# One of 16 source-row tiles of each slot in the third edge stage: one-hot products on TensorE from a table in SBUF instead of an indirect DMA

## The reference, cut to what matters

```python
row, col = (edge_index[0], edge_index[1])          # src, dst; the edges are sorted by dst
m = jnp.concatenate([x[row], x[col], edge_attr], axis=1)
h = jnp.maximum(m @ W1 + b1, 0.0)
h = jnp.maximum(h @ W2 + b2, 0.0)
h = h @ W3 + b3
s = jax.ops.segment_sum(h, col, num_segments=n)
agg_max = jax.ops.segment_max(h, col, num_segments=n)
```

## Time and profile before

| | us |
|---|---|
| median of 3 runs | 12,724.05 |
| lowest and highest of them | 12,720.05 and 12,810.73 |
| the profiled execution, its own time | 12,744.54 |
| span of that execution, first to last instruction | 12,742.7 |
| mean granted clock of TensorE in it | 0.537 of 2.4 GHz |
| third edge stage in it, from its first instruction to its last product with `yg` | 8716.3 to 12,576.2 |

### The profile page before, as it was taken

How to read it: one execution, slowest core, us unless ns; L and a number is a source line. 1 busy time by engine, 2 the same in 40 slices (tenths; PEclk the granted TensorE clock), 3 DMA queues, 4 the chain that set the end, 5 groups by cost and what they waited for, 6 DMA issues and landing times. The chain is left out here.

```text
span 12742.7 us, 117881 instructions
## 1 busy us (share of the span) xinstructions
PE 2970.5 (23%) x12074; PEld 2055.6 (16%) x12074; DVE 6179.3 (48%) x21579; ACT 1252.9 (10%) x3613; POOL 9537.5 (75%) x9956
## 2 busy tenths in 40 slices
PE   2000011111100640000000000013545545545455
PEld 2000011111100320000000000012333333333334
DVE  8877477777743432222222222224555555555555
ACT  3111111111111330000000000000101001011001
POOL 7777777777777767777777777777777777777776
PEclk6555555555555775555555555555555555555556
DMA  6444444444444432222222222222222222222221
GB/s 168 120 118 116 115 127 117 118 116 118 116 119 115 127 120 74 66 66 74 66 70 66 66 66 72 68 52 55 68 67 67 67 68 67 67 67 67 67 67 49
DMA packets 766546, 1107.81 MB, mean 87 GB/s; under 512 B 277264, under 2 KB 383263, under 8 KB 765038
## 3 DMA queue, kind: packets, MB, share of 16 engines
q0 software_dynamic: 328208, 302.76, 12.8%
q1 hardware_dynamic: 257781, 569.91, 12.3%
q10 hardware_dynamic: 179944, 229.99, 6.1%
HBM read 548.77 MB, written 553.01 MB: 86 GB/s over the span
## 5 line engine op out<-in xcount | busy, mean ns | idle before, releaser
L137 POOL DMA_INDIRECT g<-in_edge_attr,idxs x3072 | 2955.4, 962 | 938.3 <-issue 857.1
L137 POOL DMA_INDIRECT yg<-ytab,idx x3077 | 2911.6, 946 | 949.4 <-issue 920.1
L137 POOL DMA_INDIRECT msg<-Y,idx x3025 | 2874.0, 950 | 984.8 <-issue 923.5
L1600 DVE SCALAR_TENSOR_TENSOR run<-run,same,msg 128x64 f32<-128x64 f32 x3125 | 891.0, 285 | 2910.9 <-DMA msg<-Y,idx 2803.4
L611 DVE SCALAR_TENSOR_TENSOR run<-run,sameD 128x80 f32<-128x80 f32 x3072 | 907.9, 296 | 1324.3 <-DMA g<-in_edge_attr,idxs 882.5
L2023 DVE SCALAR_TENSOR_TENSOR run<-run,same,ps 128x32 f32<-128x32 f32 x3125 | 774.7, 248 | 1584.1 <-PE ps L1917 1428.7
L1156 PE MATMUL ps<-tail,before 128*128 128x64 f32 (+2 forms) x10 | 2.8, 421 | 4456.5 <-PEq L1470 3811.3
L1901 PE MATMUL ps<-ident,zx 128*128 128x128 f32 x1564 | 524.8, 439 | 1460.6 <-DMA yg<-ytab,idx 1430.5
L2006 DVE SCALAR_TENSOR_TENSOR zx<-zx,same,zs 128x32 f32<-128x32 f32 x3124 | 793.4, 254 | 135.3 <-DVE anew L1989 28.6
L615 DVE SCALAR_TENSOR_TENSOR runS<-runS,sameS,g 128x64 f32<-128x64 f32 x3072 | 852.4, 277 | 0.1
L1000 PE MATMUL ps<-hot 128*98 128x128 bf16 x3072 | 373.1, 315 | 1816.3 <-DVE hot L718 1816.3
(11 more groups left out here) (356 smaller groups left out, 5893.0 us busy)
## 6 DMA issues: line engine op xcount, KB each, us to landing
R<-run SPq DMA_DIRECT2D x390, 320.0 KB, 2.3
msg<-Y ACTq DMA_DIRECT2D x6400, 0.2 KB
msg<-Y SPq DMA_DIRECT2D x6400, 0.2 KB
R<-run SPq DMA_DIRECT2D x195, 512.0 KB, 3.0
R<-run SPq DMA_DIRECT2D x124, 800.0 KB, 5.3
v<-in_edge_attr ACTq DMA_DIRECT2D x384, 256.0 KB
yg<-ytab SPq DMA_DIRECT2D x6144, 0.1 KB
RA<-runS SPq DMA_DIRECT2D x256, 256.0 KB, 2.9
```

Source lines behind the costliest of these rows:

```text
L137: eng.indirect_dma_start(out=out, out_offset=None, in_=table, in_offset=bass.IndirectOffsetOnAxis(ap=index, axis=0)).then_inc(sem, 16)
L1600: ins_ = v.scalar_tensor_tensor(out=run[:, q, t, :], in0=prev, scalar=same[:, q, t:t + 1], in1=msg[:, q, t, :], op0=ALU.mult, op1=ALU.add)
```

## The change

Tile 4 of each of the 192 full slots (`HOT3`) is no longer fetched by GpSimd. At the start of the stage the whole `ytab` is loaded into SBUF (partition p holds its 98 nodes as 98 x 32 floats), and VectorE splits each float into three bf16 parts whose sum is the float (`prepare`). The source node of an edge is written as 7 times a key plus a rest (`HB2` = 7); the key names one of 128 x 14 groups of 7 nodes. For each slot:

- VectorE copies the keys of the tile's 128 edges (`next_key`); TensorE spreads them over all partitions by one fp32 product (`spread_key`).
- VectorE compares them with each partition's 14 group numbers into `hot`, 128 x 1792 bf16 (`one_hots`).
- TensorE multiplies 14 one-hot matrices with the three parts of the table, 42 bf16 products of 128x128 by 128x224 into one bank (`find`).
- VectorE picks one of the 7 rows of each group: a mask, a product of 128 x 224 and a sum over 7 (`pick`), into `yg`.

The steps run ahead of the slot by written order. In turn n TensorE runs `slot(n)`, then `find` for slot n + 2, then `spread_key` for slot n + 4; VectorE runs its old turn n, then `pick` for n + 2, `one_hots` for n + 3, `next_key` for n + 4. Bank 1, the second bank of stage 0, is given to the new products, so stage 0 keeps one bank. The tail is as before.

The core of the diff:

```diff
@@ edges_3, GpSimd
                 for t in range(steps):
-                    if by_rows(c, q) and t == ROW_AT3:
+                    if within(c, q) and t == HOT3 or by_rows(c, q) and t == ROW_AT3:
                         continue
                     gather(pool, yg[:, q, t * MSG:(t + 1) * MSG], k.ytab, idx[:, q, t:t + 1], got[q])
@@ edges_3, TensorE
+                        if within(c, q):
+                            pe.wait_ge(y_picked, n + 1)
...
+            def spread_key(c, q):
+                pe.wait_ge(keyed, NS3 * c + q + 1)
+                nc.tensor.matmul(psK, key[:, 0:1].to_broadcast([P, P]), k.ident[:, :], start=True, stop=True)\
+                    .then_inc(key_spread, 1)
+
+            def find(c, q):
+                pe.wait_ge(hot_ready, NS3 * c + q + 1)
+                for i in range(HN):
+                    for part in parts_y:
+                        last = nc.tensor.matmul(psP, hot[:, i, :], part[:, i * HB2 * MSG:(i + 1) * HB2 * MSG],
+                                                start=i == 0 and part is parts_y[0], stop=i == HN - 1 and part is parts_y[2])
+                last.then_inc(y_found, 1)
+
             def body(c):
                 for q in range(NS3):
                     slot(c, q, SL3)
-
-            turns(pe, CHUNKS3, body)
+                    for work, m in ((find, 2), (spread_key, 4)):
+                        if within(*after(c, q, m)):
+                            work(*after(c, q, m))
+
+            spread_key(0, 0)
+            pe.wait_ge(parts_done, 1)
+            find(0, 0)
+            spread_key(0, 1)
+            find(0, 1)
+            spread_key(0, 2)
+            spread_key(0, 3)
+            body(0)
@@ edges_3, VectorE
+            def next_key(c, q):
+                copy_at(v, key[:, :], hot_key[:, bass.ds(NS3 * c + q, 1)]).then_inc(keyed, 1)
+
+            def one_hots(c, q):
+                v.wait_ge(key_spread, NS3 * c + q + 1)
+                v.tensor_tensor(hot[:, :, :], over(psK, 1, HN), over(place[:, :], 2, P), ALU.is_equal).then_inc(hot_ready, 1)
+
+            def pick(c, q):
+                s.done(v.tensor_tensor(mask[:, :], seq[:, :], hot_in[:, bass.ds(NS3 * c + q, 1)].to_broadcast([P, HB2]), ALU.is_equal))
+                v.wait_ge(y_found, NS3 * c + q + 1)
+                s.wait(s.n)
+                s.link(v.tensor_tensor(picked[:, :, :], psP.rearrange("p (b f) -> p b f", f=MSG), over(mask[:, :], 2, MSG), ALU.mult))
+                v.tensor_reduce(yg[:, q, HOT3 * MSG:(HOT3 + 1) * MSG], picked[:, :, :].rearrange("p b f -> p f b"), AX.X, ALU.add)\
+                    .then_inc(y_picked, 1)
+
+            def prepare():
...
+                next_key(0, 0)
...
+                v.wait_ge(y_loaded, 16)
+                s.link(v.tensor_copy(parts_y[0][:, :], ysb[:, :]))
+                s.link(v.tensor_tensor(y_rest[:, :], ysb[:, :], parts_y[0][:, :], ALU.subtract))
+                s.link(v.tensor_copy(parts_y[1][:, :], y_rest[:, :]))
+                v.tensor_tensor(parts_y[2][:, :], y_rest[:, :], parts_y[1][:, :], ALU.subtract).then_inc(parts_done, 1)
+                v.wait_ge(parts_done, 1)
+                one_hots(0, 0)
+                pick(0, 0)
+                next_key(0, 1)
+                one_hots(0, 1)
+                pick(0, 1)
+                next_key(0, 2)
+                one_hots(0, 2)
+                next_key(0, 3)
+
             def body(c):
                 s.fresh()
                 for q in range(NS3):
...
                     aggregate(c, q, SL3)
                     v.wait_ge(run_ready, NS3 * c + q + 1)
                     meta(c + 1, q)
+                    for work, m in ((pick, 2), (one_hots, 3), (next_key, 4)):
+                        if within(*after(c, q, m)):
+                            work(*after(c, q, m))
```

More of the change, by code:

```diff
@@ L65 @@
 SP_ROWS, ACT_ROWS = (1, 3), (2, 4)
+HN, HB2 = 14, 7
+HOT3 = 4
 BY_ROW = (1, 2, 3, 4)
@@ L416, in edges_01 @@
                             [Xf[:, 2 * CA + h * CA // 2:2 * CA + (h + 1) * CA // 2] for h in range(2)], ctx)
-        loaded, got, stored80, storedS = ([sem(f"{s}{q}") for q in range(NQ)]
-                                          for s in ("loaded", "got", "stored80_", "storedS"))
-        added = [sem(f"added{q}") for q in range(NTAB)]
+        loaded, stored80, storedS = ([sem(f"{s}{q}") for q in range(NQ)] for s in ("loaded", "stored80_", "storedS"))
+        got, added = k.left_got, k.added
         l_srcB, l_left, l_rest, l_dst, tabs_zero, settled, consts, wzero = (
@@ L1803, in edges_3 @@
                              "run_ready3", "vsteps3"))
+        ysb, y_rest = sb("ysb", [P, NB * MSG]), sb("y_rest", [P, NB * MSG])
+        parts_y = [sb(f"y_part{i}", [P, NB * MSG], BF16) for i in range(3)]
+        seq_i, place_i = sb("seq3_i", [P, HB2], I32), sb("place3_i", [P, HN], I32)
+        seq, place = sb("seq3", [P, HB2]), sb("place3", [P, HN])
+        hot_src, hot_key, hot_in = (sb(f"hot3_{s}", [P, NS3 * CHUNKS3]) for s in ("src", "key", "in"))
+        key, mask = sb("key3", [P, 1]), sb("mask3", [P, HB2])
+        hot, picked = sb("hot3", [P, HN, P], BF16), sb("picked3", [P, HB2, MSG])
+        y_loaded, seqs_made, keyed, key_spread, hot_ready, y_found, y_picked, parts_done = (
+            sem(s) for s in ("y_loaded3", "seqs_made3", "keyed3", "key_spread3", "hot_ready3", "y_found3", "y_picked3",
+                             "parts_done3"))
+        psK, psP = k.ps[:, 1, 0:P], k.ps[:, 1, 2 * P:2 * P + HB2 * MSG]
         e32 = ins["edge_attr_32"].rearrange("(p t) f -> p (t f)", p=P)
@@ L1809, in ps, with after, within @@
         def ps(stage, q):
-            return k.ps[:, LANES * stage + q % LANES, 0:W]
+            return k.ps[:, LANES * stage + (q % LANES if stage else 0), 0:W]
+        def after(c, q, m):
+            return c + (q + m) // NS3, (q + m) % NS3
+        def within(c, q):
+            return not (isinstance(c, int) and c >= CHUNKS3)
         def groups(steps):
@@ L1839, in row_tile @@
                 list_rows(c + 1)
+            sp.dma_start(ysb[:, :], k.ytab.rearrange("(p b) f -> p (b f)", p=P)).then_inc(y_loaded, 16)
             list_rows(0)
@@ L1857, in _ @@
         def _(pool):
+            pool.iota(seq_i[:, :], pattern=[[1, HB2]], base=0, channel_multiplier=0).then_inc(seqs_made, 1)
+            pool.iota(place_i[:, :], pattern=[[1, HN]], base=0, channel_multiplier=HN).then_inc(seqs_made, 1)
             def slot(c, q, steps):
@@ L1881, in slot @@
                 pe.wait_ge(loaded[q], 32 * c + 32)
-                if behind:
-                    pe.wait_ge(turned_c, n + 1 - LANES)
+                if lags(c, q, 1):
+                    pe.wait_ge(turned_c, n)
                 for a, w in groups(steps):
@@ L1897, in slot @@
                             pe.sem_clear(by_row)
-                        pe.wait_ge(got[q], 16 * (SL3 - (q == ROW_SLOT3)) * c + 16 * (steps - by_rows(c, q)))
+                        if within(c, q):
+                            pe.wait_ge(y_picked, n + 1)
+                        pe.wait_ge(got[q], 16 * (SL3 - 1 - (q == ROW_SLOT3)) * c + 16 * (steps - within(c, q) - by_rows(c, q)))
                     for g, _ in groups(steps):
@@ L1923, in body @@
                     slot(c, q, SL3)
-            turns(pe, CHUNKS3, body)
+                    for work, m in ((find, 2), (spread_key, 4)):
[9 more added lines that the diff above has]
+            body(0)
+            with pe.Fori(1, LAST) as c:
+                body(c)
+            body(LAST)
             for q, steps in enumerate(TAILS3):
@@ new lines, in prepare @@
+            def prepare():
+                s.done(v.tensor_copy(hot_src[:, :], k.src_i[:, 0:CHUNKS3 * CH3].rearrange("p (n t) -> p n t", t=SL3)[:, :, HOT3]))
+                v.wait_ge(seqs_made, 2)
+                s.done(v.tensor_copy(seq[:, :], seq_i[:, :]))
+                s.done(v.tensor_copy(place[:, :], place_i[:, :]))
+                s.wait(s.n)
+                s.link(v.tensor_scalar(hot_key[:, :], hot_src[:, :], 1.0 / HB2, -3.0 / HB2, ALU.mult, ALU.add))
+                s.link(v.tensor_scalar(hot_key[:, :], hot_key[:, :], 1.5 * 2.0 ** 23, None, ALU.add))
+                s.link(v.tensor_scalar(hot_key[:, :], hot_key[:, :], -1.5 * 2.0 ** 23, None, ALU.add))
+                next_key(0, 0)
+                s.done(v.scalar_tensor_tensor(out=hot_in[:, :], in0=hot_key[:, :], scalar=-1.0 * HB2, in1=hot_src[:, :],
+                                              op0=ALU.mult, op1=ALU.add))
+                v.wait_ge(y_loaded, 16)
[12 more added lines that the diff above has]
+                next_key(0, 3)
@@ L2043, in _ @@
             spread_z(0, 0, SL3)
-            turns(v, CHUNKS3, body)
+            prepare()
+            body(0)
+            with v.Fori(1, LAST) as c:
+                body(c)
+            body(LAST)
             s.fresh()
@@ L2330, in build @@
         k.row_got = [ctx.enter_context(nc.semaphore(f"row_got{r}")) for r in range(RING)]
```

(2 more changed lines are left out.)

## The result

The changed kernel takes 13,140.5 us (13,135.1 to 13,142.0, 4 runs), the kernel before 12,722.1 (12,718.8 to 12,810.7, 4 runs): a ratio of 1.031, 95% interval 1.027 to 1.036. It is slower by 3.1%, with 192 gathers fewer. The profiled execution after has a span of 13,133.3 us. Single executions of some of the kernels are some 60 to 90 us longer than the rest (12,810.7 above; 13,220.1 in experiment 3, where the extra time lies ahead of the third edge stage), and one of the ten of experiment 6 took 14,907.3 us, for a cause that no trace shows.

What follows compares the result with a forecast made beforehand. GpSimd bounded the kernel before; after, the closed loop of VectorE and TensorE does. 187 slots x (22.0 - 19.71) = +428, start +33, end -45: +416 us, 13,140 us (+3.3%); forecast's own range 12,860 to 13,460, 80% range 12,640 to 13,640.

Steps and rivals of the forecast that it cites:

- What bounds before: Third edge stage before the change: GpSimd sets the pace at 19.7 us a slot, TensorE having 7.4 us to spare.
- The wait decides: TensorE waits before `spread_key` for VectorE's key, written behind the finished slot's aggregate: 3 to 6 us idle a slot.
- VectorE's answer 10.85 us: VectorE's time from W3's end to the key: 7.55 us old part plus 3.3 us new part.
- TensorE's slot: TensorE from the key wait to W3's end: 13.8 us at 1.2 GHz, 8.4 us at 2.4 GHz.
- Slot time 22.0: Steady-stage slot with clock rising late in W1 and identity products: 24.95 - 0.3 - 2.65 = 22.0 us, against 19.71.
- Start +33, end -45: Ends of the third edge stage: table load and preparation add 33 us, last slots without key wait save 45.
- Rival 1: TensorE's clock stays at 1.2 GHz wherever the path needs it: 13,715 us, 12 in 100.
- rival 2: TensorE's clock stays at 2.4 GHz throughout, 19.3 us a slot: 12,625 us, within 1%, 8 in 100.
- Rival 4: A new piece costs more than its row, such as 42 unhidden weight loads: above 13,460 us, 7 in 100.
- Rival 3: Slot falls under GpSimd's 18.46 us, so the removed gather counts in full: -240 us, 12,485 us, 6 in 100.
- The port warning of the Trainium skill: Some VectorE instructions hold a port GpSimd needs; gathers beside one-hots take 956 ns against 946, not the bound.
- the loop: VectorE's answer and TensorE's slot alternating through the key wait: 24.95 us at 1.2 GHz, 19.3 at 2.4.

Runs made afterwards that it cites:

- experiment 3: Changed kernel with GpSimd gathering tile 4 again into a spare buffer nobody reads: 13,137.7 us.
- experiment 6: Changed kernel with 28 more unread bf16 products of 512 columns behind `find` in each slot: 12,690.9 us.
- experiment 1: Changed kernel with TensorE spreading the key three slots ahead in place of four, before `find`: 12,522.7 us, ratio 0.984 to the kernel before.
- experiment 4: Changed kernel with the key three slots ahead and tile 4 gathered again into a spare buffer: 12,734.7 us, ratio 0.9996 to the kernel before.
- experiment 5: Changed kernel with VectorE writing each slot's one-hots twice: 13,505.3 us.
- experiment 7: Two edits of the changed kernel on a stalling chip: `find` and `pick` left out, tile 4 gathered, 17,903 us; half the one-hots, 18,278; kernel before 18,430.

## Why the prediction was right, point by point

- **What bounds before.** Shown by experiments 1 and 4: with the same gathers as before the slot takes 19.7 us and the kernel the same time, although all of the work is added; with one gather less it takes 18.4.
- **The wait decides.** Shown by experiments 1 and 3 to 5, and by the undisturbed slots of experiment 7. TensorE idles 6.7 us a slot before the key; the forecast of 3 to 6 was too short, since I let `find` run in part at 1.2 GHz (up to 8.05 us), and it took 4.19 in each. GpSimd's spare time, 22.02 - 18.46 = 3.6 us, is near the 3.5 forecast; the views put 2.9 of it down to ScalarE's indices, not to TensorE.
- **VectorE's answer 10.85 us.** 10.75 (10007.88 to 10018.63). Its terms: one-hots 2.01 as forecast; the product 0.39; the sum over 7 takes 0.53, not 0.38, partly beside its neighbour.
- **TensorE's slot.** From 10018.63 to 10029.69 (the end of the next W3 at 10028.56 + 1.13) it is 11.1 us, and 11.3 on the mean of the 158 slots, between 8.4 and 13.8. Both clocks stand where they were forecast: low from the key through W1 and at least the first five identity products, high for W2, W3 and `find`.
- **Slot time 22.0.** 22.02. The mechanism was right, but the hundredths are luck. The sum doesn't add up as written: the savings that it names are 0.95 + 0.91 + 1.1 = 2.96 us, and it takes off 0.3 + 2.65, so the 0.3 us for `find` ending late is either inside the 1.1 or makes the slot 21.7. The measured halves are 10.7 for VectorE's answer (0.1 less than forecast) and 11.3 for TensorE's slot (0.15 more than the 11.15 left for it), and the two errors cancel. That the clock rises late in the run of W1 and the identity products was read from one slot of before, and the 1.1 us "on the rest" was a guess. In 71 of 158 slots it rises only between the last identity product and W2: a little later, and W2 would have been slow too.
- **Start +33, end -45.** Measured +28.5, and 379.7 - 187 x (22.02 - 19.71) = -52 for the end. `find` ran at 5.7 us there in place of 8; the conversion passes took 1.8 and 3.4 us in turn, 10.5 in place of 14; but the load was waited for nowhere, as VectorE had other things to do until 8712.
- **Rival 1 (1.2 GHz throughout)** and **rival 2 (2.4 throughout)** are both refuted for the changed kernel by its timeline; rival 2's 19.3 us was nearly reached when the rest was filled (experiment 6: 19.45).
- **Rival 4 (a new piece costs more than its row)** did not come about: `find` took 4.19 us against 4.1 forecast for 2.4 GHz, so its weight loads are hidden.
- **Rival 3 (the gather counts in full)** did not hold for the changed kernel. Its time was nearly reached by another way, when the loop was opened and not shortened: 12,485 by the rival, 12,523 in experiment 1.
- **The port warning of the Trainium skill** (SBUF — State Buffer, "Who interferes with whom"): no run here shows it; the gathers take 944 ns beside one-hots, picks and sums.

## What to carry to other kernels

When work is taken from the bound engine and spread over others, first list each new wait with the instruction that answers it, and follow that one back through its engine's written order: here a key known from the start stood behind the aggregate of the slot just finished, and two engines that had overlapped took turns. Looking ahead by one slot more is not safer: work of slot n + 3 handed over a turn ago is ready, work of n + 4 handed over at the end of this turn is not. The kernel with the key three ahead is the fastest of the study, 1.6% (1.1 to 2.1) under the kernel before; after that GpSimd's gathers are the bound again.

## What the runs showed of the hardware

- In each slot of the changed kernel's steady stage TensorE's clock was down behind the rest and up again before W2; only the place of the rise moved, which spread single slots over 21.2 to 22.5 us while the mean of 80 stayed at 22.02 (22.04 with 14 products in place of 42). On this the Trainium skill (TensorE: Matmul & The Clock Gate, "HAM oscillation — how this bites in real kernels") says that waits between bursts send the clock down. The trace agrees: behind each rest of 6.6 to 6.8 us the transposes take 1.06 us and not 0.60. The rest cost 2.6 us of the 22.0 by way of the clock (experiment 6).
- Products that nobody reads, put where TensorE would rest, raised the granted clock from 0.78 to 0.98 and made the kernel 450 us faster.
- The same kernel took 12,722 to 12,728 us on some chips and some 18,400 on two others. There single row DMA issues take up to 1.4 us on SyncE; the median is 0.23 on both kinds, and the longest in the third edge stage of the changed kernel is 0.35. Why these chips stall is not known.
